# Last layer of a fused four-layer kernel: a fixed phase between the search for row maxima and the attention, and the last value product of a unit moved into the next unit

## What is computed

```
xn = layernorm(x)
q, k, v = heads(xn @ Wq.T), heads(xn @ Wk.T), heads(xn @ Wv.T)
attn = softmax(where(causal, q @ k.T * 0.25, -inf))
x = x + (attn @ v) @ Wo.T + sqrt((xn @ cos(..))**2 + (xn @ sin(..))**2)
```

## Time and profile before

| | us |
|---|---|
| median of 3 runs (3840.07 to 3855.26) | 3845.64 |
| span of the profiled execution | 3867.5 |
| of it the stretch from 2850 on, in which the last layer's search and attention run | 1018 |
| PE, DVE, ACT, POOL busy over the span | 91%, 64%, 45%, 30% |

### The profile page before, as it was taken

One profiled execution on the slowest core, in us unless ns is written; L12 is line 12 of the kernel. 1 busy time (PEld: TensorE's weight loads), 2 busy tenths in 40 slices (PEclk: granted clock), 3 DMA queues, 4 the chain that ended last, 5 costly groups with the idle time before them and its releaser, 6 DMA issues.

```text
span 3867.5 us, 47778 instructions
## 1 busy us (share of the span) xinstructions
PE 3519.2 (91%) x16468; PEld 2089.1 (54%) x16468; DVE 2473.4 (64%) x6381; ACT 1730.0 (45%) x3237; POOL 1164.8 (30%) x1190
## 2 busy tenths in 40 slices
PE   8899999968898988989878999998899999999998
PEld 7677777734555545545546667676543333433332
DVE  4444443455788988889865443443568788678774
ACT  2234443322234423343344544443346666666667
POOL 0322222151355555555542322223211111011111
PEclk7799999988899999999989999999889899999999
DMA  3244445321466666666750000000101011111100
GB/s 109 73 165 168 177 180 180 128 66 71 136 204 193 216 211 194 197 204 197 212 187 3 0 1 1 1 1 9 38 20 31 20 23 34 31 34 27 32 18 23
DMA packets 107154, 368.87 MB, mean 95 GB/s; under 512 B 27248, under 2 KB 41088, under 8 KB 96928
## 3 DMA queue, kind: packets, MB, share of 16 engines
q0 software_dynamic: 57664, 302.82, 24.3%
q1 hardware_dynamic: 48160, 60.90, 5.6%
q10 hardware_dynamic: 1088, 2.10, 0.2%
HBM read 322.59 MB, written 17.69 MB: 88 GB/s over the span
## 4 chain that ended last, share of the span: by engine, by line
PE 66%; DVE 21%; ACT 6%; issue 4%; another core or an unknown queue 2%; POOL 1%; DMA 0%; POOLq 0%; DVEq 0%; SPq 0%; ACTq 0%
PE ps L184 51%; PE ps L2636 6%; DVE pm L2784 4%; PE ps L1507 2%; DVE mi L1642 2%; DVE gathB L1719 2%; DVE ps L2787 2%; DVE hacc L1682 2%; ACT P L2917 1%; PE ps L2126 1%; DVE mx L1638 1%; PE ps L556 1%; PE ps L581 1%; PE ps L546 1%
## 5 line engine op out<-in xcount | busy, mean ns | idle before, releaser
L2917 ACT ACTIVATE P<-ps 128x512 f32<-128x512 f32 (+3 forms) x1280 | 587.3, 548 | 214.1 <-PE ps L184 212.0
L2784 DVE TENSOR_REDUCE pm<-ps 128x1 f32<-128x512 f32 x768 | 484.6, 684 | 113.3 <-PE ps L184 113.0
L1860 POOL DMA_INDIRECT gathB<-in_tab,idx x256 | 282.9, 1105 | 357.6 <-PE ps L1507 287.4
L184 PE MATMUL ps<-QS,KS 49*128 49x512 f32 (+3 forms) x1280 | 333.8, 422 | 16.2 <-DVE pm L2784 12.6
L1860 POOL DMA_INDIRECT gathA<-in_tab,idx x256 | 268.7, 1049 | 203.2 <-DVE mx L1638 125.5
L184 PE MATMUL ps<-KS,QS 48*128 48x512 f32 (+3 forms) x1280 | 309.8, 430 | 16.0 <-DVE pm L2787 5.9
L2974 POOL TENSOR_SCALAR_AFFINE_SELECT P<-P 128x256 f32<-128x256 f32 x256 | 103.8, 409 | 709.9 <-ACT P L2917 709.0
L2636 PE MATMUL ps<-P,Va 128*32 128x512 f32 (+3 forms) x2560 | 309.7, 557 | 5.8 <-POOL P L2974 2.9
L184 PEld LDWEIGHTS ps<-QS,KS 49*128 49x128 f32 x1280 | 158.2, 190 | 225.0 <-DVE pm L2784 81.8
L184 PEld LDWEIGHTS ps<-KS,QS 48*128 48x128 f32 x1280 | 145.5, 191 | 212.8 <-DVE pm L2784 66.2
L2787 DVE CUSTOM_DVE_ANT_0 ps<-ps,past 128x128 f32<-128x128 f32 (+3 forms) x512 | 240.1, 515 | 26.6 <-PE ps L184 24.6
(11 more groups left out here) (390 smaller groups left out, 7002.8 us busy)
## 6 DMA issues: line engine op xcount, KB each, us to landing
ys_sorted<-moe SPq DMA_DIRECT2D x71, 128.0 KB
KS<-hi SPq DMA_DIRECT2D x256, 32.0 KB, 1.9
QS<-hi SPq DMA_DIRECT2D x256, 32.0 KB, 1.9
gathA<-in_tab,idx POOLq DMA_INDIRECT x256
gathB<-in_tab,idx POOLq DMA_INDIRECT x256
KS<-lo SPq DMA_DIRECT2D x128, 32.0 KB, 1.9
QS<-lo SPq DMA_DIRECT2D x128, 32.0 KB, 2.0
out<-xT SPq DMA_DIRECT2D x8, 512.0 KB, 3.2
```

Source lines behind the costliest of these rows:

```text
L184: m = pe.matmul(out, w, x, start=start and i == 0, stop=stop and i == len(pairs) - 1, skip_group_check=True)
L1860: pool.indirect_dma_start(out=(GA, GB)[half][:, h, :], out_offset=None, in_=d[f"tab{half}"], in_offset=bass.IndirectOffsetOnAxis(ap=idx[t ...
L2784: v = dve.tensor_reduce(m, p, AX.X, ALU.max)
L2917: act.activation(P_[:, hh, off:BW], psx.tile("s2", j, n, kt, pr, hh)[:, off:BW], ACT.Exp).then_inc(*psx.emptied(MN.act, "s2", j, n, kt, pr ...
```

## The change

The generators of search and attention are given a common phase. A search step always advances the clock by 0.125 and the chunks of a key tile by 0.03, 0.14 and 0.08, so a key tile always lasts 0.25, and attention starts at 6.02 where search steps lie on multiples of 0.125. Per key tile the order is then: search step, score pair, score pair, search step, value product. Before, a unit's extra yields (after `qk`, after `max`, at the end of a unit) made the two sides drift against each other. These extra yields are gone: `qk` and `max` are emitted in the chunk of their search step. The last value product of a unit is kept in `tail.before` and emitted at the first key tile of the next unit. In the tail the copy to `osb` moves to the second `step()`, `sum` from the first to the fourth, the logarithm from the first to the fifth and the exponential from the second to the sixth, `out` from the sixth and seventh to the eighth and ninth, and DVE's two additions from the sixth and seventh to the ninth and tenth. On POOL the `On` of the preceding unit moves, in a unit with n = 0, from behind the masks of key tile 0 to behind those of key tile 2. The copies of `v` for the second sequence spread over (3, 3) and the first key tile of (4, 0). No instruction of the kernel is added or removed.

```diff
@@ -2486,7 +2486,8 @@
-PHASE, PROJECT, SEEK, VALUES, ATTEND = (0.0, 0.055), (0.2, 0.3), 1.0, (4.2, 0.12), 6.0
+PHASE, PROJECT, SEEK, VALUES, ATTEND = (0.0, 0.055), (0.2, 0.3), 1.0, (4.2, 0.12), 6.02
+SEARCH, STEP = 0.125, (0.03, 0.14, 0.08)
 def at_pace(chunks, step):
     for _ in chunks:
@@ -2495,12 +2496,13 @@
 def everything(qk, phase, prep, v, main, last):
     def seek():
         for u in range(NJ * NQ):
-            yield from at_pace(prep(*divmod(u, 4)), (u % 4 + 1) / (8 * (u % 4) + 10))
+            yield from at_pace(prep(*divmod(u, 4)), SEARCH)
         yield from at_pace(last(), 0.1)
     def attend():
         for u in range(NJ * NQ):
-            yield from at_pace(main(*divmod(u, 4)), (u % 4 + 1) / (12 * (u % 4) + 13))
+            for i, _ in enumerate(main(*divmod(u, 4))):
+                yield STEP[i % 3]
     def project():
         for n in range(2):
@@ -2607,51 +2609,48 @@
                     pe.wait_all(psx.freed("s", j, pr, qt, c, hh))
                     chain(pe, p[hh][:, 0:w], [(Q[rs, pr, qs], K[rs, pr, c * 512:c * 512 + w])]).then_inc(
                         *PP.pe.tick("s", j, pr, qt, c, hh))
-                yield
                 step += 1
                 also = beside(n, step)
                 if also == "qk" and ahead(j, n)[0] < NJ:
                     pe_qk(pe, *ahead(j, n))
                 if also == "max" and preceding(j, n)[0] >= 0:
                     pe_max(pe, *preceding(j, n))
-                if also:
-                    yield
+                yield
 def pe_last(pe):
     pe_max(pe, NJ - 1, NQ - 1)
     yield
+def pe_values(pe, j, n, kt, off):
+    o_ = po.fill("o", j, n) if kt == 0 else po.tile("o", j, n)
+    if kt == 0:
+        pe.wait_all(po.freed("o", j, n))
+    pe.wait_ge(*PP.act.has("v", j // 4, 14))
+    pe.wait_ge(*(MN.pool.has("causal", j, n, kt, 1) if kt >= 4 * n else MN.act.has("s2", j, n, kt, 1, 1)))
+    for hd in range(4):
+        h = 4 * (j % 4) + hd
+        m = pe.matmul(o_[32 * hd:32 * hd + 32, off:BW], Va[:, kt, h * 17:h * 17 + 32],
+                      Pb[2 * (kt % 2) + hd // 2][:, hd % 2, off:BW], start=kt == 0, stop=kt == 4 * n + 3,
+                      skip_group_check=True)
+    m.then_inc(*MN.pe.tick("pv", j, n, kt))
+
 def pe_main(pe, j, n, tail, v):
-    g = j % 4
     Q, K = QS[j % 2], KS[j % 2]
-    def pv(n, kt, off):
-        o_ = po.fill("o", j, n) if kt == 0 else po.tile("o", j, n)
-        if kt == 0:
-            pe.wait_all(po.freed("o", j, n))
-        pe.wait_ge(*PP.act.has("v", j // 4, 14))
-        pe.wait_ge(*(MN.pool.has("causal", j, n, kt, 1) if kt >= 4 * n else MN.act.has("s2", j, n, kt, 1, 1)))
...
-
-    def finish(n):
+    def finish():
+        yield from nothing(3)
         p = psx.fill("sum", j, n)
         pe.wait_ge(*MN.act.has("o", j, n))
         pe.wait_all(psx.freed("sum", j, n))
         chain(pe, p[:, :], [(selS[:, :, :].rearrange("p a b -> p (a b)"), osb[:, :])]).then_inc(*MN.pe.tick("sum", j, n))
-        yield from nothing(5)
+        yield from nothing(4)
         for m in range(2):
             p = psx.fill("attn", j, n, m)
             pe.wait_ge(*MN.pool.has("on", j, n))
             pe.wait_all(psx.freed("attn", j, n, m))
-            chain(pe, p[:, :], [(WoP[:, g, m * 128:(m + 1) * 128], On[:, :])]).then_inc(*MN.pe.tick("out", j, n, m))
+            chain(pe, p[:, :], [(WoP[:, j % 4, m * 128:(m + 1) * 128], On[:, :])]).then_inc(*MN.pe.tick("out", j, n, m))
             yield
-    before = None
     for kt in range(4 * n + 4):
         off = max(0, (kt - 4 * n) * 128)
         for pr in range(2):
@@ -2664,21 +2663,19 @@
                 chain(pe, s2[hh][:, off:BW], [(K[rs, pr, kt * 128:(kt + 1) * 128],
                                                Q[rs, pr, n * BW + off:(n + 1) * BW])]).then_inc(
                     *MN.pe.tick("s2", j, n, kt, pr, hh))
+            tail.step()
             yield
-            tail.step()
-            if pr == 1 and before is not None:
-                pv(n, *before)
-                if kt % 2 and kt > 2:
-                    next(v, None)
-                yield
-        before = (kt, off)
-    yield
-    pv(n, *before)
-    for _ in v:
-        pass
+        if tail.before is not None:
+            pe_values(pe, *tail.before)
+        tail.before = (j, n, kt, off)
+        if kt % 2 and kt > 2:
+            next(v, None)
+        if (n, kt) == (0, 0):
+            for _ in v:
+                pass
+        yield
     tail.drain()
-    tail.gen = finish(n)
-    yield
+    tail.gen = finish()
 def pe(pe):
     pe.wait_ge(*W3A.total())
@@ -2689,8 +2686,11 @@
         yield from nothing(TURN)
         yield from pe_phase(pe)
+    second = pe_v(pe, 1)
     pe_all(pe, everything(lambda j, n: pe_qk(pe, j, n), phase, lambda j, n: pe_prep(pe, j, n), lambda: pe_v(pe, 0),
-                        lambda j, n: pe_main(pe, j, n, tail, pe_v(pe, 1) if (j, n) == (3, 3) else iter(())), lambda: pe_last(pe)))
+                        lambda j, n: pe_main(pe, j, n, tail, second if (j, n) in ((3, 3), (4, 0)) else iter(())),
+                        lambda: pe_last(pe)))
+    pe_values(pe, *tail.before)
     tail.drain()
@@ -2789,24 +2789,22 @@
                     v.then_inc(*psx.emptied(PP.dve, "s", j, pr, qt, c, hh))
                 if (qt, c) == (4 * n + 3, n):
                     dve_maxima(dve, j, n, pr)
-                yield
                 step += 1
                 also = beside(n, step)
                 if also == "qk" and ahead(j, n)[0] < NJ:
                     dve_qk(dve, *ahead(j, n))
                 if also == "max" and preceding(j, n)[0] >= 0:
                     dve_max(dve, *preceding(j, n))
-                if also:
-                    yield
+                yield
 def dve_last(dve):
     dve_max(dve, NJ - 1, NQ - 1)
     yield
-def dve_main(dve, j, n, tail, v):
-    def finish(n):
+def dve_main(dve, j, n, tail):
+    def finish():
         b = j // 4
-        yield from nothing(5)
+        yield from nothing(8)
         for m in range(2):
             dve.wait_ge(*MN.pe.has("out", j, n, m))
             dve.wait_ge(*x_before(4 * b + n))
@@ -2817,18 +2815,11 @@
     for kt in range(4 * n + 4):
         for pr in range(2):
+            tail.step()
             yield
-            tail.step()
-            if pr == 1 and kt:
-                if kt % 2 and kt > 2:
-                    next(v, None)
-                yield
-    yield
-    for _ in v:
-        pass
+        yield
     tail.drain()
-    tail.gen = finish(n)
-    yield
+    tail.gen = finish()
 def dve(dve):
     dve_start(dve)
@@ -2886,16 +2877,17 @@
 def act_prep(act, j, n):
     for step in range(1, 8 * n + 9):
-        yield
-        also = beside(n, step)
-        if also == "qk" and ahead(j, n)[0] < NJ:
+        if beside(n, step) == "qk" and ahead(j, n)[0] < NJ:
             act_qk(act, *ahead(j, n))
-        if also:
-            yield
+        yield
 def act_main(act, j, n, tail, v):
-    def finish(n):
-        act.wait_ge(*MN.pool.has("on", *((j, n - 1) if n else (j - 1, 3))))
+    def finish():
+        yield
+        act.wait_ge(*MN.pool.has("on", *preceding(j, n)))
+        act.wait_ge(*MN.pe.has("pv", j, n, 4 * n + 3))
+        act.activation(osb[:, :], po.tile("o", j, n)[:, :], ACT.Copy).then_inc(*po.emptied(MN.act, "o", j, n))
+        yield from nothing(3)
         act.wait_ge(*MN.pe.has("sum", j, n))
         act.activation(inv[:, :], psx.tile("sum", j, n), ACT.Ln).then_inc(*psx.emptied(MN.act, "sum", j, n))
         yield
@@ -2916,21 +2908,16 @@
                 act.wait_ge(*MN.pe.has("s2", j, n, kt, pr, hh))
                 act.activation(P_[:, hh, off:BW], psx.tile("s2", j, n, kt, pr, hh)[:, off:BW], ACT.Exp).then_inc(
                     *psx.emptied(MN.act, "s2", j, n, kt, pr, hh))
+            tail.step()
             yield
-            tail.step()
-            if pr == 1 and kt:
-                if kt % 2 and kt > 2:
-                    next(v, None)
-                yield
-    yield
-    for _ in v:
-        pass
-    act.wait_ge(*MN.pool.has("on", *((j, n - 1) if n else (j - 1, 3))))
-    act.wait_ge(*MN.pe.has("pv", j, n, 4 * n + 3))
+        if kt % 2 and kt > 2:
+            next(v, None)
+        if (n, kt) == (0, 0):
+            for _ in v:
+                pass
+        yield
     tail.drain()
-    act.activation(osb[:, :], po.tile("o", j, n)[:, :], ACT.Copy).then_inc(*po.emptied(MN.act, "o", j, n))
-    tail.gen = finish(n)
-    yield
+    tail.gen = finish()
 def act(act):
     tail = Tail()
@@ -2939,8 +2926,10 @@
         yield from act_weights(act)
         yield from act_phase(act)
+    second = act_v(act, 1)
     act_all(act, everything(lambda j, n: act_qk(act, j, n), phase, lambda j, n: act_prep(act, j, n), lambda: act_v(act, 0),
-                        lambda j, n: act_main(act, j, n, tail, act_v(act, 1) if (j, n) == (3, 3) else iter(())), lambda: nothing(1)))
```

(21 more changed lines are left out.)

## The result

The changed kernel takes 4068.97 us (median of 4 runs, 4059.43 to 4084.5) against 3848.27 for the kernel before: 1.0565 times as long, with a 95% interval of 1.0527 to 1.0603, or 5.7% slower. Forecast was 3921, with a range up to 3966. The direction was right and the size was not: the kernel lost 221 us where 75 were forecast.

The account below looks back on a forecast made before the run. The stage was taken as bound by round trips through the ring of seven banks, 2.7 us per key tile. Three new tail waits and `qk`/`max` meetings gave +10 us per j, times 7.5: 3845.6 + 75 = 3921 us, range 3872 to 3966.

Parts of the forecast that it names:

- Plain tiles: Plain key tiles in the new order: still 2.7 us, no gain, with -0.2 to +0.2 per tile open.
- The three new waits: Unit's tail: logarithm's bank in tile 2 costs 1.2 us, first `out` on `On` in tile 3 1.1, addition in tile 4 1.8.
- The sum over a j: Units n = 0 to 3 together: 131.3 us against 120.6 in the trace, taken as +10 us per j.
- the 2.4 for `max`: `max` waits for `qk`'s bank until `lo` frees it, value product behind it: 0.8 us in three of four units.
- Tile 1, with `sum`: Key tile 1 of a unit: `sum` stands behind both score pairs and waits for `osb`; the tile takes 3.4 us.
- The carry: Unit's last value product, moved into the next unit, no longer waits for the last mask; first key tile takes 2.1 us.
- The meeting of `qk` and the second `out`: In units with n = 1, the first score pair waits for the addition behind `lo`; tile 0 takes 5.6 us.
- The count of js: The loss per j counts 7.5 times, because the last key tiles have no search beside them: +75 us.
- The clock: Rival, 17%: PE's clock drops some 5 us per unit in tiles 2 to 4, +42 us on top: 3963 us.
- Faster: Rival, 10%: the new waits don't bind; a j takes about 115 us, 5.5 below 120.6, -40 us: 3805 us.
- No change: Rival, 15% in all: half of the prices come true, +10 to +35 us at most, down to 0; point 3850 us.

Follow-up runs that it names:

- the first two experiments on the tail: Changed kernel with one number changed each: DVE's additions one step earlier, 3944.54 us (1.0280); logarithm and exponential one step earlier, 3950.60 us (1.0295).
- the kernel with both numbers: Changed kernel with DVE's two additions and ACT's logarithm and exponential each one step earlier: 3853.53 us, 1.0049 times the kernel before.
- the first experiment: Changed kernel plus five matmuls per unit (three where n = 0) adding zeros inside the three waits: 3974.43 us, 1.0358 times the kernel before.

## Why the prediction was right and wrong

**Plain tiles: right.** In the changed kernel they take 2.64 to 2.71 us, as the earlier trace rows had it, and nothing was gained.

**The three new waits: right, at their places and nearly in their size.** The logarithm's bank cost 1.72 us of idle PE and a tile of 4.1 (3.9 forecast), `On` 0.98 and 4.3 (4.3), the addition 1.74 and, where the clock did not fall, 5.2 (5.0). Each of the first two experiments on the tail took away the wait that it was to take away, and both together brought a j to 121.2 us at the full clock, against 121.0 for the kernel before.

**The sum over a j: the first step that failed, 10 us and not 14.** At the full clock a j of the changed kernel takes 135.1 us (the middle value of each of the 40 tiles over the units in which the clock did not fall, and the shortest in five tiles where it always did); I had worked out 131.3, and of the 10.7 us above the 120.6 of the kernel before I took 10. The kernel before has 121.0 at the full clock, so the loss is 14.

The error is not in the three waits. I had them at 1.2, 1.1 and 1.8 us, together 12 in three units and 1.5 where n = 0, or 13.5 per j. Compared tile by tile with the kernel with both numbers, the kernel with extra matmuls loses 1.4, 0.7 and 1.8 in tiles 2, 3 and 4 and 2.3 in all where n = 0, and that is the 14. What failed is the rest of the tiles. Without the waits and the 2.4 for `max` I had 115 us for a j, that is, I had counted on a gain of 5.5 from the new order and the carry; the kernel with both numbers has 121.2, so there was none. Tile 1, with `sum`, takes 3.8 and not 3.4 in three of four units. The carry is worth 0.7 us per j at the full clock. The meeting of `qk` and the second `out` leaves a tile of 6.7 us in n = 0 even without the waits. And moving `max` away gained 0.5 us per j, not 2.4.

The three waits themselves end 0.1 to 0.2 us later than I had them, because the logarithm takes 0.60 and the addition 0.68 us where I put 0.5 and 0.6, and 0.05 pass from there to the matmul.

**The count of js: wrong.** I took 7.5 js, since the last tiles have no search beside them. But for j = 7 the kernel with extra matmuls took 126.0 us against 113.9 before, nearly the loss of the other js. Eight times 14 is 113 of the 122 us of waits and order that the first experiment leaves, where I had forecast 75; the other 9 stay open. Ahead of the stage, between the first search pair and the first score pair, the changed kernel lost 7 us more, which I had put at 0. With the waits as measured, 122 + 7, and no change of the clock, the forecast would have been 3975 us, already outside its range.

**The clock: the step that failed by most.** The forecast let the clock stay as it was and gave a fall to a rival of 17%. I argued against it that the granted clock was 0.96 with a wait in nearly every tile. Those waits show as idle of 0.19 to 0.23 us, with PE at work on either side. The new ones are of 1.0 to 1.7 us, three of them within 11 us, in tiles of which PE works about half to seven tenths by my count. One kind was no evidence on the other: the kernel with both numbers still has short ones (58 in the stage), and 0.96. The term that I had put at nothing measured 82 us, of some 146 by which the forecast was too low. The price was right: 0.28 us lost per us at the lower clock, from the earlier trace rows, against 82 us for (384 - 89) us by the first experiment, which is 0.28 as well. The amount was not: I gave the rival 5 us per unit, 150 in all, and there were 300. (In the kernel without the carry that price leaves 7 us open, so it need not hold everywhere.) The Trainium skill, "TensorE: Matmul & The Clock Gate", section "A second HAM failure mode: psum-queue depth-cycling", says that frequent small pauses from cycling through PSUM banks make the clock swing. The traces agree only in part: the small pauses went with 0.96 before and in the kernel with both numbers, and it took the long waits on the ring to bring it to 0.84.

**The rivals.** *Faster* fell, and its calculation was too rosy even with the waits gone: I had 115 us for a j without them, and the kernel with both numbers has 121.2. The tiles that I had too short are those named under the sum over a j. *No change* fell too. *The clock* came true, on top of more waits than I had counted.

## What to carry to other kernels

When PE runs through a ring of banks that all kinds of work share, follow each bank for one turn of the ring: who takes it next, and what stands ahead of its reader in that engine's queue. A step that frees a bank must come no later than the step that refills it; one position cost 2.7% here, in both phases. And count a wait of PE twice if it is long, as those of 1.0 to 1.7 us here: once for its time, and once for the lower clock that can follow it, which here made up 82 of 204 us of the stage's loss.

## What the runs showed of the hardware

Matmuls that do nothing useful can make a kernel faster. Put into idle time of PE, they raised the granted clock of the stage from 0.84 to 0.96 and took 2% off the changed kernel, with each wait ending at the same time. The clock was 82 of 204 us, or 40% of the stage's loss; the prediction had given it 42 us, with a chance of 17%.

Short pauses of PE for DVE's reductions, nearly all of 0.2 to 0.3 us, stood in the kernel before (94 in the stage) and in the kernel with both numbers (58), both at a granted clock of 0.96. The waits of 1.0 to 1.7 us, three within 11 us, went with 0.84.
